# Selective scan stage: units of all four channel tiles, 512-wide copies of the turned states, a state carried by a VectorE copy

## The reference

```python
D_MODEL, D_STATE, D_CONV, D_INNER, DT_RANK = (256, 16, 4, 512, 64)   # x: (2, 2048, 256)
def step(h, inp):
    dt_t, u_t, B_t, C_t = inp
    A_bar = jnp.exp(dt_t[..., None] * A)
    h = A_bar * h + dt_t[..., None] * B_t[:, None, :] * u_t[..., None]
    y = jnp.sum(h * C_t[:, None, :], axis=-1)
    return (h, y)
```

## Time and profile before

| | us |
|---|---|
| median of 3 runs (lowest, highest) | 3929.85 (3924.43, 3930.31) |
| the profiled execution's own time | 3933.48 |
| its span, first to last instruction | 3931.7 |
| scan stage, first load issued to the store of the last unit issued | 290 to 1020 |
| busy in the span: PE, DVE, ACT, POOL | 3406, 2863, 2320, 901 |

### The profile page before, as it was taken

One profiled execution on the slowest core, in us unless ns is written; L12 is line 12 of the kernel. 1 busy time (PEld: TensorE's weight loads), 2 busy tenths in 40 slices (PEclk: granted clock), 3 DMA queues, 4 the chain that ended last, 5 costly groups with the idle time before them and its releaser, 6 DMA issues. The chain is left out here.

```text
span 3931.7 us, 57533 instructions
## 1 busy us (share of the span) xinstructions
PE 3406.4 (87%) x18410; PEld 1684.6 (43%) x18410; DVE 2862.9 (73%) x4259; ACT 2320.4 (59%) x4496; POOL 900.9 (23%) x770
## 2 busy tenths in 40 slices
PE   6866888888698887999786999999999999995896
PEld 2325666666455554777431222222222222223664
DVE  7757999999555554545468888888888888863665
ACT  4557999999400000222123888888788888883342
POOL 2227988888200000000021000000000000001100
PEclk9888999999799998999886999999999999997998
DMA  3339855663211101020221010000000000001101
GB/s 118 130 126 188 160 144 149 146 140 91 82 47 30 47 30 46 19 61 17 68 78 51 13 24 14 19 14 20 23 16 20 13 20 18 14 3 57 32 21 43
DMA packets 204870, 231.48 MB, mean 59 GB/s; under 512 B 67971, under 2 KB 135171, under 8 KB 203845
## 3 DMA queue, kind: packets, MB, share of 16 engines
q1 hardware_dynamic: 204628, 228.35, 22.2%
HBM read 160.93 MB, written 67.37 MB: 58 GB/s over the span
## 5 line engine op out<-in xcount | busy, mean ns | idle before, releaser
L1659 DVE TENSOR_REDUCE attn_part_max<-attn_pM 128x1 f32<-128x1024 f32 x1024 | 1204.7, 1219 | 163.9 <-PE attn_pM L1714 160.7
L1639 ACT ACTIVATE attn_probs<-attn_pE 128x512 f32<-128x512 f32 x2048 | 1089.9, 597 | 206.9 <-PE attn_pE L1763 202.5
L1763 PE MATMUL attn_pE<-attn_q,attn_k_exp 128*128 128x512 bf16 x2048 | 629.3, 386 | 31.0 <-ACT attn_q L1611 24.6
L514 POOL TENSOR_TENSOR scan_dbu<-scan_du,scan_b_all 128x2048 f32<-128x2048 f32 x128 | 579.9, 4540 | 73.6 <-DVE scan_h L576 69.9
L1734 PE MATMUL attn_pA<-attn_probs,attn_v 128*32 128x512 f32 x4096 | 561.2, 605 | 0.0
L528 ACT ACTIVATE scan_hcT<-scan_hT,scan_c_t 128x256 f32<-128x256 f32 x1024 | 522.6, 663 | 0.0
L576 DVE TENSOR_TENSOR_SCAN scan_h<-scan_abar,scan_h,scan_dbu 128x512 f32<-128x512 f32 x384 | 487.2, 1280 | 29.6 <-POOL scan_dbu L514 11.3
L543 ACT ACTIVATE scan_abar<-scan_delta,scan_decay 128x512 f32<-128x512 f32 x512 | 450.1, 879 | 23.7 <-DVE scan_h L576 23.6
L591 PE MATMUL scan_hT<-scan_ident,scan_h 128*128 128x128 f32 x2048 | 368.5, 287 | 89.0 <-ACT scan_hcT L528 66.3
L1763 PEld LDWEIGHTS attn_pE<-attn_q,attn_k_exp 128*128 128x128 bf16 x2048 | 138.9, 97 | 608.6 <-ACT attn_probs L1639 466.6
L928 PE MATMUL moe_pP<-moe_w_qkv,moe_xT 128*128 128x384 f32 x1024 | 355.0, 508 | 10.6 <-DVE moe_acc L818 10.6
(11 more groups left out here) (267 smaller groups left out, 3861.2 us busy)
## 6 DMA issues: line engine op xcount, KB each, us to landing
scan_b_all<-mid_BC SPq DMA_DIRECT2D x64, 1024.0 KB, 10.2
attn_q<-mid_q_parts SPq DMA_DIRECT2D x224, 64.0 KB, 2.4
mid_uT<-front_uT SPq DMA_DIRECT2D x8, 1024.0 KB, 6.4
mid_gT<-front_gT SPq DMA_DIRECT2D x8, 1024.0 KB, 9.0
mid_dT<-front_dT SPq DMA_DIRECT2D x8, 1024.0 KB, 4.3
scan_delta<-mid_dT SPq DMA_DIRECT2D x16, 512.0 KB, 3.8
scan_u_in<-mid_uT SPq DMA_DIRECT2D x16, 512.0 KB, 4.8
scan_g<-mid_gT SPq DMA_DIRECT2D x16, 512.0 KB, 3.8
```

The costliest lines, as they stand in the source:

```text
L514: nc.gpsimd.tensor_tensor(dbu[:, p % NDBU, :, :, :], du_pair, b_pair, ALU.mult).then_inc(dbu_ready, 1)
L1639: nc.scalar.activation(probs[:, kt % 4, h, :], pE[:, bank(item), :], ACT.Exp, scale=SCALE).then_inc(exp_done, 1)
L1659: nc.vector.reduce_max(part_max[:, h, j, i:i + 1], pM[:, m % 2, :], AXIS_X).then_inc(max_read, 1)
L1763: nc.tensor.matmul(pE[:, bank(item), :], k_exp[:, par, kt * 128:(kt + 1) * 128], q[:, qc, h, :], start=True, stop=True).then_inc(e_psum, 1)
```

## The change

- A unit is now all four channel tiles of one chunk: 8 units, 16 groups each, four scans a group. delta, u, gate and du double in size, b is loaded 8 x 4 times, not 16 x 4.
- dbu is made for one state index and four tiles, still 128x2048 and 128 times. The du product is 128x2048, 8 times.
- A tile of 128 tokens of all four channel tiles is turned into one full PSUM bank (hT has two), and is copied by one instruction of 128x512. There are eight buffers for the copies, and the copy of tile i stands six steps behind (LAG). y_acc has four banks.
- h has three buffers of four tiles, not one for each n. A new VectorE instruction, `keep_state`, copies the last column of the four tiles (128x4, stride 512) to `states`, for every group, and the scans of later chunks read their first state there. It stands behind the first scan of the next group.
- TensorE holds back the additions of a new unit for seven tiles (HOLD), until VectorE has multiplied the last unit's four banks by the gate, at step 9 (FINAL_AT), and then does two additions a tile until it has caught up.
- C's rows are read into the gate's buffer, so SP waits for them to be turned (c_psum) before it loads gates.

```diff
@@ -408,42 +408,37 @@
 def selective_scan(nc, a):
 
 
-    MP = 2
-    UNITS = B * (NDI // MP) * CPB
+    UNITS = B * CPB
     G_UNIT = NS
-    K_UNIT = NS * MP
-    PAIRS = NS // 2
+    K_UNIT = NS * NDI
+    I_UNIT = NS * TPC
     BQ = NS // 4
-    NDBU, NHC = 3, 3
+    NDBU, NH, NHC = 3, 3, 8
     LAST = UNITS * G_UNIT
-    D_AT = (6, 10)
-    FINAL_AT = 4
-
-    def place(u):
...
         c_t = s.sb("c_t", [128, NT, NS])
+        states = s.sb("states", [128, NS, NDI])
         b_all = s.sb("b_all", [128, 2, NS, CH])
-        delta, u_in, g, du = (s.sb(n, [128, 2, MP, CH]) for n in ("delta", "u_in", "g", "du"))
-        dbu = s.sb("dbu", [128, NDBU, 2, MP, CH])
-        h = s.sb("h", [128, NS, MP, CH])
-        hcT = s.sb("hcT", [128, NHC, TPC, MP * 128])
-        y_acc = s.ps("y_acc", [128, MP, CH])
-        hT = s.ps("hT", [128, 4, CH])
+        delta, u_in, g, du = (s.sb(n, [128, 2, NDI, CH]) for n in ("delta", "u_in", "g", "du"))
+        dbu = s.sb("dbu", [128, NDBU, NDI, CH])
+        h = s.sb("h", [128, NH, NDI, CH])
+        hcT = s.sb("hcT", [128, NHC, NDI * 128])
+        y_acc = s.ps("y_acc", [128, NDI, CH])
+        hT = s.ps("hT", [128, 2, CH])
         abar = s.ps("abar", [128, 2, CH])
-        c_rows = h[0:NS, NS - T // (MP * CH):NS, :, :].rearrange("p n m c -> p (n m c)")
+        c_rows = g[0:NS, :, :, :].rearrange("p a m c -> p (a m c)")
...
-                load_gate(0)
                 for i in range(4):
                     load_b(1, i)
+                sp.wait_ge(c_psum, 1)
+                load_gate(0)
...
-                    for i in range(PAIRS):
+                    for n in range(NS):
                         pool.wait_ge(du_ready, u + 1)
-                        pool.wait_ge(b_in[u % 2][i // 2], (u // 2 + 1) * 16)
-                        p = u * PAIRS + i
-                        at_least(pool, scan_done, (p - NDBU + 1) * 2 * MP)
-                        du_pair = du[:, u % 2, :, :].unsqueeze(1).broadcast_to([128, 2, MP, CH])
-                        b_pair = b_all[:, u % 2, 2 * i:2 * i + 2, :].unsqueeze(2).broadcast_to([128, 2, MP, CH])
-                        nc.gpsimd.tensor_tensor(dbu[:, p % NDBU, :, :, :], du_pair, b_pair, ALU.mult).then_inc(dbu_ready, 1)
-                        if i == PAIRS // 2 and u + 1 < UNITS:
+                        pool.wait_ge(b_in[u % 2][n // BQ], (u // 2 + 1) * 16)
+                        G = u * NS + n
+                        at_least(pool, scan_done, (G - NDBU + 1) * NDI)
+                        b_row = b_all[:, u % 2, n, :].unsqueeze(1).broadcast_to([128, NDI, CH])
+                        nc.gpsimd.tensor_tensor(dbu[:, G % NDBU, :, :], du[:, u % 2, :, :], b_row, ALU.mult).then_inc(dbu_ready, 1)
+                        if n == NS // 2 and u + 1 < UNITS:
                             make_du(u + 1)
...
-                def evacuate(G, half):
+                def evacuate(i):
+                    G, tile = divmod(i, TPC)
                     u, n = divmod(G, G_UNIT)
-                    b, mp, j = place(u)
-                    act.wait_ge(turned, (G + 1) * MP)
-                    if half == 0:
-                        at_least(act, sum_done, 2 * (G - NHC + 1))
-                    for i in range(2):
-                        tile = 2 * half + i
-                        nc.scalar.activation(hcT[:, G % NHC, tile, :], hT[:, 2 * (G % 2) + half, i * 256:(i + 1) * 256], ACT.Copy,
-                                             scale=c_t[:, b * (L // TILE) + j * TPC + tile, n:n + 1]).then_inc(hc_ready, 1)
+                    act.wait_ge(turned, i + 1)
+                    at_least(act, sum_done, i - NHC + 1)
+                    nc.scalar.activation(hcT[:, i % NHC, :], hT[:, i % 2, :], ACT.Copy, scale=c_t[:, u * TPC + tile, n:n + 1]).then_inc(hc_ready, 1)
...
                     at_least(act, scan_done, k - 1)
-                    nc.scalar.activation(abar[:, k % 2, :], delta[:, u % 2, m, :], ACT.Exp, scale=decay[:, mp * MP + m, n:n + 1]).then_inc(abar_ready, 1)
+                    nc.scalar.activation(abar[:, k % 2, :], delta[:, u % 2, m, :], ACT.Exp, scale=decay[:, m, n:n + 1]).then_inc(abar_ready, 1)
...
-                    if G >= 2:
-                        evacuate(G - 2, m)
-                for G in (LAST - 2, LAST - 1):
-                    for half in range(2):
-                        evacuate(G, half)
+                    if k >= LAG:
+                        evacuate(k - LAG)
...
+                def keep_state(G):
+                    dve.wait_ge(scan_done, (G + 1) * NDI)
+                    nc.vector.tensor_copy(states[:, G % NS, :], h[:, G % NH, :, CH - 1]).then_inc(state_kept, 1)
+
+                for k in range(LAST * NDI):
+                    G, m = divmod(k, NDI)
                     u, n = divmod(G, G_UNIT)
-                    if k == (NS - T // (MP * CH)) * MP:
-                        dve.wait_ge(c_psum, 1)
                     dve.wait_ge(abar_ready, k + 1)
-                    if k % 4 == 0:
-                        dve.wait_ge(dbu_ready, k // 4 + 1)
-                    at_least(dve, turned, k - K_UNIT + 1)
-                    if place(u)[2]:
-                        dve.wait_ge(scan_done, k - K_UNIT + 1)
-                    state = h[:, n, m, CH - 1:CH] if place(u)[2] else 0.0
-                    nc.vector.tensor_tensor_scan(h[:, n, m, :], abar[:, k % 2, :], dbu[:, (k // 4) % NDBU, n % 2, m, :], state, ALU.mult, ALU.add).then_inc(scan_done, 1)
-                    if u and k % K_UNIT == FINAL_AT - 1:
+                    if m == 0:
+                        dve.wait_ge(dbu_ready, G + 1)
+                        at_least(dve, turned, (G - NH + 1) * TPC)
+                        at_least(dve, state_kept, G - NH + 1)
+                    if u % CPB:
+                        dve.wait_ge(state_kept, G - NS + 1)
+                    state = states[:, n, m:m + 1] if u % CPB else 0.0
+                    nc.vector.tensor_tensor_scan(h[:, G % NH, m, :], abar[:, k % 2, :], dbu[:, G % NDBU, m, :], state, ALU.mult, ALU.add).then_inc(scan_done, 1)
+                    if m == 0 and G:
+                        keep_state(G - 1)
+                    if u and k % K_UNIT == FINAL_AT:
                         finish(u - 1)
...
-                def turn(k):
-                    G, m = divmod(k, MP)
-                    pe.wait_ge(scan_done, k + 1)
-                    for half in range(2):
-                        if m == 0:
-                            at_least(pe, hc_ready, 4 * (G - 2) + 2 * (half + 1))
-                        for i in range(2):
-                            t = (2 * half + i) * 128
-                            last = nc.tensor.transpose(hT[:, 2 * (G % 2) + half, i * 256 + m * 128:i * 256 + (m + 1) * 128], h[:, G % G_UNIT, m, t:t + 128], ident[:])
+                def turn(i):
+                    G, tile = divmod(i, TPC)
+                    pe.wait_ge(scan_done, (G + 1) * NDI)
+                    at_least(pe, hc_ready, i - 1)
+                    for m in range(NDI):
+                        last = nc.tensor.transpose(hT[:, i % 2, m * 128:(m + 1) * 128], h[:, G % NH, m, tile * 128:(tile + 1) * 128], ident[:])
                     last.then_inc(turned, 1)
...
+                added = 0
+                for i in range(LAST * TPC):
+                    G, tile = divmod(i, TPC)
                     u, n = divmod(G, G_UNIT)
-                    if k == MP:
+                    if i == 1:
                         pe.wait_ge(c_ready, 1)
-                    turn(k)
-                    if m == 0 and G >= 2:
-                        add(G - 2, 1)
-                    if m == 1 and G >= 1:
-                        add(G - 1, 0)
-                    if m == 1 and n in D_AT:
+                    turn(i)
+                    ready = u * I_UNIT if u and i % I_UNIT < HOLD else i - 1
+                    for _ in range(2):
+                        if added < ready:
+                            add(added)
+                            added += 1
+                    if tile == TPC - 1 and n in D_AT:
                         skip(u, D_AT.index(n))
```

More of the change, by code:

```diff
@@ L582, in _, with add @@
             def _(pe):
[L583 to L591 removed]
+                def turn(i):
+                    G, tile = divmod(i, TPC)
+                    pe.wait_ge(scan_done, (G + 1) * NDI)
+                    at_least(pe, hc_ready, i - 1)
+                    for m in range(NDI):
+                        last = nc.tensor.transpose(hT[:, i % 2, m * 128:(m + 1) * 128], h[:, G % NH, m, tile * 128:(tile + 1) * 128], ident[:])
                     last.then_inc(turned, 1)
[L594 removed]
+                def add(i):
+                    G, tile = divmod(i, TPC)
                     u, n = divmod(G, G_UNIT)
[L596 to L603 removed]
+                    pe.wait_ge(hc_ready, i + 1)
+                    if n == 0 and tile == 0:
+                        at_least(pe, y_ready, u * NDI)
+                    for m in range(NDI):
```

(2 more changed lines are left out.)

58 lines of the change are left out of this document (21 added, 37 removed).

## The result

The changed kernel takes 4280.2 us (median of four runs, 4279.4 to 4280.9), the kernel before 3927.7 in the same session (3924.4 to 3930.3): a ratio of 1.090, 95% interval 1.088 to 1.092. Forecast were 4294 us and a range of 4240 to 4335. The profiled execution has a span of 4277.3 us against 3931.7, so the two traces differ by 345.6 us, and the medians by 352.5.

What follows compares the result with a forecast made beforehand. Before, ScalarE set the scan stage's pace (1.34 us a scan, 5.36 a group); groups would now take 8.29 or 8.11. Last scan +360.9, tail +3.6: +364.5, 4298.0 for the profiled run, so 4294 us (+9.3%); range 4240 to 4335.

Steps and rivals of the forecast that it cites:

- The copy waits for the running product: Scan stage: each state COPY on VectorE that meets a GpSimd product waits until it ends, mean near 3.6 us; chance 0.86.
- copy free: Rival: the state COPY doesn't wait and takes 0.1 us, groups take 4.79 or 4.75, total 3855 us; chance 0.08.
- The period: Scan stage, groups 3 to 125: 8.29 us a group with a state, 8.11 without, where it took 5.36.
- First three groups: Start of the scans: GpSimd has two products ahead, copies wait only for their rest, about 21.4 us.
- near ties: Seven du places and the third group: copy at 9.38, du's end at 9.26 us behind the boundary.
- the -28 of the range: Range's allowance for near ties at du places and third group: up to 8 waits of 3.5 us freed.
- Unit ends: Seven unit ends inside the loop: four gate products for two, 2.43 us each with overlap, 17.0 in all.
- The stage's start: Before the first scan: 1 MB more to load adds 3.0 us, first scan at 308.7 instead of 305.7.
- Between first and last scan: Scan stage: sum of groups, unit ends and du products, 1068.1 us, so the last scan ends at 1376.8.
- TensorE at nothing: Scan stage: TensorE's work costed at nothing, since it fits into the group even at its lower clock, 6.8 us.
- The tail: Behind the last scan: six copies for two pairs of groups, four gate products for two, larger store: +3.6 us.
- the signs: List of what would show the forecast in the trace, among them units of 64 scans near 133 us.

## Why the prediction held, step by step

- **The copy waits for the running product.** Right: 3.62 us, forecast "near 3.6", ending with the product. The rival "copy free" (3855, 0.08) named the right price of the other case: kernels without the wait took 3854 to 3858.
- **The period.** 8.26 with a state (between the starts of two products, 702.61 to 710.87) and 8.09 without (367.13 to 375.22), forecast 8.29 and 8.11. Over 123 groups 3 us too many.
- **First three groups and the near ties.** Forecast 21.4 us, measured 17.3: the copy of the second group, at 316.77, came when one product had just ended and took 0.14 us. Of the seven du places, which I priced at +0.8 each and called near ties, five took 0.7 more and two (the units without a state) went the other way: their copy was free, 7 us together. All of it was in the -28 of the range.
- **Unit ends.** The row below shows four gate products of 2.45 us together, which make the group 10.64 us for 8.26, 2.38 more; forecast 2.43.

```profile
715.33 1.27 DVE L566 TENSOR_TENSOR_SCAN scan_h<-scan_abar,scan_states,scan_dbu 128x512 f32<-128x512 f32 x1
716.52 2.45 DVE L549 TENSOR_TENSOR scan_g<-scan_y_acc,scan_g 128x512 f32<-128x512 f32 x4
718.89 3.62 DVE L566 TENSOR_TENSOR_SCAN scan_h<-scan_abar,scan_states,scan_dbu 128x512 f32<-128x512 f32 x3
```

- **The stage's start.** Two things lie in this term, how long the loads take and where the stage begins, and I asked only about the first. The first scan came at 303.51, not at 308.7. The rows of the changed kernel, and then of the kernel before:

```profile
283.44 0.37 SPq L463 DMA_DIRECT2D scan_a_log<-in_a_log_d  x1
```

```profile
303.51 2.34 DVE L566 TENSOR_TENSOR_SCAN scan_h<-scan_abar,scan_dbu 128x512 f32<-128x512 f32 x2 [38.03 <-POOL scan_dbu L507]
```

```profile
290.06 0.37 SPq L470 DMA_DIRECT2D scan_a_log<-in_a_log_d  x1
...
305.67 2.34 DVE L576 TENSOR_TENSOR_SCAN scan_h<-scan_abar,scan_dbu 128x512 f32<-128x512 f32 x2 [33.57 <-POOL scan_dbu L514]
```

  From the stage's first issue to its first scan it takes 20.07 us; in the trace of before 305.67 - 290.06 = 15.61. That is +4.5, where I gave +3.0. But the ten other traces with units of four tiles have 18.6 to 19.6 us here, and the kernel before with the copy has 16.2, so the change's own part is some 2.4 to 4.5 us and the 3.0 was about right. The stage began 6.6 us earlier, however. Nothing in the change touches what is ahead of it, and in the 13 traces of this case the first issue falls anywhere between 283.2 us and 291.2, so this is a matter of the single execution. I took the stage's position in one run as given, and it was luck that this moved the total by no more.
- **Between first and last scan** 1053.5 us, forecast 1068.1. The difference of 14.6 is 4.1 (first groups), 7.0 (two free copies), 3 (period) and 0.5 (unit ends and du products).
- **TensorE at nothing.** Right in both cases: at a granted clock of 0.82 in the changed kernel it waited for the scans and for ScalarE's copies, and without the pauses the clock was 0.95 and it still stayed behind VectorE.
- **The tail.** +4.5 for +3.6.

In sum: start -6.6 + 4.5, between the scans 1053.5 - 710.2 = +343.3, behind them +4.5: 345.6 us. The forecast was +364.5, and 14.6 of its 18.9 too many are in the scans' own sum. The unit of 64 scans took 135.3 us with a state (16 x 8.26 + 2.4 + 0.7), where the signs said "near 133": a slip in that line, since the sum's own terms give 16 x 8.29 + 2.43 + 0.8 = 135.9.

What was weak is the reason, not the number. The prediction asked which sort a COPY of four elements is and listed L83, with two inputs, among the instructions that wait, but then went by the one-source rows alone. When it came to a remedy, that reading led me to prefer a form that waits just as long (4282 us).

## What to carry over

When a small instruction is put on an engine beside a long one of another engine, price it by what is left of that long instruction at the place where it comes, not by its own length: here 3.62, 1.30 or 0.14 us for the same four elements behind the first, third or fourth scan. Look then for the form that doesn't wait (a reduce over one element, an input from PSUM, single elements, or ScalarE), since a position that works hangs on 0.2 us. And look at the least and greatest duration of an instruction beside its mean: a span of 134 to 4512 ns for one form is a wait, however busy the engine is called.

## What was not expected of the hardware

- A TENSOR_TENSOR of 128x4 with both inputs in SBUF waits for a GpSimd product like a COPY does (median 3.62 us, greatest 4.50), while a TENSOR_REDUCE of the same elements never does (greatest 0.139).
- A waiting copy is as a rule not held up by a second GpSimd instruction that is queued right behind the running one: 119 of 120 ended with the first (0.07 us after it in the row shown). One waited for three instructions in a row, 8.15 us.
- A 128x4 ACTIVATE between two 512-wide ones delays the next by 0.09 us, for a recorded mean of 0.31.
- In the changed kernel, with TensorE pausing some microseconds in every group, its granted clock was 0.82; in the six kernels where no such copy waits it was 0.95 to 0.99 (600 to 900 us). It cost nothing here, since TensorE had time: it was busy 382 of 600 us.
